# Stages two to six of a two-layer decoder in one block, with stage three rewritten and six weight pieces split inside it

## The reference, cut to what matters

```python
# stage three: one dense product, and one of four rank-8 LoRA experts per token
h = layernorm(x)
logits = h @ gate_w.T + expert_bias
e = argmax(logits)                              # one expert per token
x = x + h @ W_up.T + (h @ lora_A[e].T) @ lora_B[e].T
# stage four: a gated polynomial of seven terms and a gated feed-forward of width 1248
h = layernorm(x)
x = x + sum over d of value_d(h) @ W_down[d]    # 7 terms, then 10 blocks of silu(h Wg) * (h Wu)
```

## Time and profile before

| | before |
|---|---|
| median of 3 runs | 1293.69 us |
| the profiled execution | 1293.84 us, span 1291.9 us |
| TensorE busy | 1138.2 us, 88% of the span |
| VectorE, ScalarE, GpSimd busy | 749.5, 442.6, 399.7 us |
| mean granted TensorE clock | 0.935 |
| stage two | about 203 to 391 us |
| stage three | about 391.6 to 478 us |
| stage four | about 478.5 to 929 us |
| stages five and six | to 1291.9 us |

### The profile page before, as it was taken

The page is one execution under the profiler, slowest core; times in us unless marked ns, Lnnn a source line. Parts: engine busy times, 40 slices in busy tenths (PEclk is TensorE's granted clock), DMA queues, the critical chain, the costliest instruction groups (busy, mean ns, idle before and its releaser), DMA issues.

```text
span 1291.9 us, 24210 instructions
## 1 busy us (share of the span) xinstructions
PE 1138.2 (88%) x9396; PEld 602.5 (47%) x9396; DVE 749.5 (58%) x1308; ACT 442.6 (34%) x773; POOL 399.7 (31%) x339
## 2 busy tenths in 40 slices
PE   6798986988887978898999999999978799999993
PEld 3454443666664434344344444444545444444441
DVE  6767774788886874635721531531379833646456
ACT  4565662555541113421111211211256532223230
POOL 2345485878820010009800000000043400415053
PEclk9886885999998998998999999999989999999997
DMA  6000100111101003422200000000000000000000
GB/s 219 3 3 2 28 2 27 41 39 41 36 3 40 0 10 100 137 75 75 68 1 1 1 0 0 0 1 1 1 10 9 1 1 1 17 16 32 0 33 33
DMA packets 28911, 35.73 MB, mean 28 GB/s; under 512 B 5850, under 2 KB 20467, under 8 KB 28692
## 3 DMA queue, kind: packets, MB, share of 16 engines
q1 hardware_dynamic: 27410, 34.40, 8.3%
q10 hardware_dynamic: 1410, 0.06, 0.1%
HBM read 30.10 MB, written 4.19 MB: 27 GB/s over the span
## 4 chain that ended last, share of the span: by engine, by line
PE 47%; DVE 10%; ACT 3%; issue 2%; POOL 1%; DVEq 0%; POOLq 0%; ACTq 0%
PE p_up L113 9%; PE p_up L114 8%; PE p_up L115 8%; PE p_y L113 7%; PE p_y L114 7%; PE p_y L115 7%; DVE e_den L2122 1%; ACT wd_hi L2171 1%; DVE e_top L2112 1%; PE p_up L107 1%; DVE d_xn L100 1%; DVE e_bias L2115 1%; DVE d_h_low L1848 1%; DVE d_term L1839 1%; DVE d_xt_low L156 1%
## 5 line engine op out<-in xcount | busy, mean ns | idle before, releaser
L1848 DVE TENSOR_TENSOR d_h_low<-d_hf,d_h_high 128x512 f16<-128x512 f32 (+1 forms) x40 | 32.9, 822 | 204.5 <-ACT d_h_high L1916 204.5
L113 PE MATMUL p_up<-d_xt_high,wd_hi 128*128 128x512 f16 (+1 forms) x352 | 134.4, 382 | 1.5 <-PE p_y L115 1.5
L114 PE MATMUL p_up<-d_xt_low,wd_hi 128*128 128x512 f16 (+1 forms) x352 | 134.4, 382 | 0.0
L115 PE MATMUL p_up<-d_xt_high,wd_lo 128*128 128x512 f16 (+1 forms) x352 | 134.2, 381 | 0.0
L113 PE MATMUL p_y<-wd_hi,d_h_high 128*128 128x512 f16 (+1 forms) x272 | 104.4, 384 | 8.9 <-DVE d_h_low L1848 8.9
L114 PE MATMUL p_y<-wd_lo,d_h_high 128*128 128x512 f16 (+1 forms) x272 | 104.6, 385 | 0.0
L115 PE MATMUL p_y<-wd_hi,d_h_low 128*128 128x512 f16 (+1 forms) x272 | 104.4, 384 | 0.0
L129 POOL TENSOR_SCALAR ve<-mv 128x4 f32<-128x4 f32 x8 | 2.3, 292 | 314.5 <-DVE mv L188 314.5
L165 ACT ACTIVATE d_sg<-p_up 128x512 f32<-128x512 f32 (+1 forms) x40 | 23.8, 594 | 211.8 <-PE p_up L115 211.8
L429 POOL TENSOR_TENSOR a_pt_low<-a_ex,a_pt_high 128x1024 f16<-128x1024 f32 x32 | 68.3, 2135 | 81.1 <-ACT a_pt_high L918 81.0
L2380 DVE TENSOR_TENSOR d_h_low<-d_hf,d_h_high 128x512 f16<-128x512 f32 x32 | 27.5, 859 | 71.0 <-ACT d_h_high L2469 71.0
(11 more groups left out here) (327 smaller groups left out, 2988.7 us busy)
## 6 DMA issues: line engine op xcount, KB each, us to landing
wd_raw<-in_w_d SPq DMA_DIRECT2D x16, 616.0 KB, 3.7
wd_raw<-in_w_f SPq DMA_DIRECT2D x8, 578.0 KB, 3.7
X<-in_x SPq DMA_DIRECT2D x4, 1024.0 KB, 12.3
wd_lo<-in_ctx_t SPq DMA_DIRECT2D x128, 32.0 KB
out_x<-wd_raw SPq DMA_DIRECT2D x16, 256.0 KB, 2.0
wd_lo<-in_ctx SPq DMA_DIRECT2D x32, 64.0 KB, 2.4
wd_raw<-in_w_c SPq DMA_DIRECT2D x1, 1096.0 KB, 12.5
wd_hi<-in_Wo SPq DMA_DIRECT2D x1, 1024.0 KB
```

What stands on the lines that cost most here:

```text
L113: nc.tensor.matmul(ps, st[0], mv[0], start=start, stop=False)
L114: nc.tensor.matmul(ps, st[0], mv[1], start=False, stop=False)
L115: return nc.tensor.matmul(ps, st[1], mv[0], start=False, stop=stop)
L1848: nc.vector.tensor_tensor(hid[1][0:n, d % NH, :], value, hid[0][0:n, d % NH, :], ALU.subtract).then_inc(h_ready, 1)
```

## The change

Stages two to six become one block (`stages_bcdef`), with shared buffers and PSUM banks, and the loops of GpSimd and SP in stage two and of all engines in stage three are written out.

- **Stage two's end.** GpSimd makes rstd and -mean x rstd for stage three chunk by chunk inside stage two (`rstd_next`). ScalarE normalises stage three's tiles 0 and 1 at n = 28 and 30, TensorE transposes them ahead of the last `attend`, VectorE makes their low halves ahead of the last `norm_o`.
- **Stage three** (`part_c`). Normalisation moves to ScalarE (one activation with scale and bias). The gate has five operations for eight. z becomes f16 in high, high and low parts (ScalarE `high_z`, VectorE `low_z`), 96 columns, is transposed by one f16 matmul with an identity, copied by ScalarE (`copy_z`) and multiplied with an f16 lora of high, low and high rows: one pass for delta. TensorE's order is turn_z(t-1), trans(t+1), delta(t-1), products(t).
- **Six weight pieces of stage four** are split in stage three, after t = 2, 4, ..., 12: ScalarE writes the high half and then scales the raw piece in place (`high_first`), GpSimd subtracts (`low_first`). SP fetches pieces 0 and 1 at the end of stage two's fetches.
- **Stage three's end.** VectorE normalises stage four's tiles 0 and 1 at t = 14 and interleaves the rest with the last updates; TensorE's transposes (`turn_next`) stand between its last steps.
- **Stage four.** The ten other pieces are split at d = 2, 4, 6 and 7 to 13, behind the d's value on both engines and no longer ahead of it. Two normalisations of the next chunk come at d = 13 and 14, the other two ahead of all low halves. Stage five's folding of weights moves behind up(0), its first keys behind up(1).
- **Stage six** has the same new order of `prepare`, two normalisations at f = 5 and 6.

```diff
+EARLY = (2, 4, 6, 8, 10, 12)
...
+                def rstd_next(c):
+                    tiles = slice(TC * c, TC * c + TC)
+                    pool.wait_ge(stats, TC * c + TC)
+                    pool.wait_ge(vb_ready, VB * (min(TC * c + 2 * TC, NT) + 2))
+                    rstd_steps(nc, pool, held, tiles, held.rs_c + 2 * c)
+                    pool.wait_ge(held.rs_ready, held.rs_c + 2 * c + 2)
+                    nc.gpsimd.tensor_tensor(held.nmr[:, tiles], held.mv[:, tiles, 0], held.rstd[:, tiles, 0],
+                                            ALU.mult).then_inc(held.nmr_ready, 1)
+                    pool.wait_ge(held.nmr_ready, 2 * c + 1)
+                    nc.gpsimd.tensor_scalar(held.nmr[:, tiles], held.nmr[:, tiles], -1.0, None,
+                                            ALU.mult).then_inc(held.nmr_ready, 1)
+                for c in range(1, NC):
                     for i in range(TC):
                         tile(c, i, True)
-
-            @block.vector
-            def _(v):
+                    rstd_next(c - 1)
+                rstd_next(NC - 1)
...
+                    if n == N + 1:
+                        p.c.low(v, 0)
+                        p.c.low(v, 1)
...
+                    if n in (N - 4, N - 2):
+                        p.c.norm(act, (n - N + 4) // 2)
...
+                    if n == N:
+                        p.c.trans(pe, 0)
+                        p.c.trans(pe, 1)
...
+    def gpsimd(pool, weights):
+        for c in range(NC):
+            for q, t in enumerate(EARLY):
+                if TC * c <= t - 2 < TC * c + TC:
+                    weights(q)
+            rstd_chunk(nc, pool, held, c, stats, held.rs_d + 2 * c)
...
+    def gate(v, t):
+        k = 4 * t
+        v.wait_ge(aux_ready, t + 1)
+        nc.vector.scalar_tensor_tensor(logit[:], p_aux(t)[:, 0:EX4], 1.0 / (XS * WS), held.ebias[:],
+                                       ALU.mult, ALU.add).then_inc(gated, 1)
+        v.wait_ge(gated, k + 1)
+        nc.vector.tensor_reduce(top[:, 0:1], logit[:], AX.X, ALU.max).then_inc(gated, 1)
+        v.wait_ge(gated, k + 2)
+        nc.vector.scalar_tensor_tensor(pick[:], logit[:], top[:, 0:1], held.rank[:],
+                                       ALU.is_equal, ALU.mult).then_inc(gated, 1)
+        v.wait_ge(gated, k + 3)
+        nc.vector.tensor_reduce(top[:, 1:2], pick[:], AX.X, ALU.max).then_inc(gated, 1)
+        v.wait_ge(gated, k + 4)
+        nc.vector.scalar_tensor_tensor(
+            z32[:], pick[:].rearrange("p (e b) -> p e b", b=1).broadcast_to([128, EX4, R8]), top[:, 1:2],
+            p_aux(t)[:, EX4:CG].rearrange("p (e r) -> p e r", e=EX4), ALU.is_equal, ALU.mult).then_inc(zp_ready, 1)
+
+    def low_z(v, t):
+        v.wait_ge(zh_ready, t + 1)
+        nc.vector.scalar_tensor_tensor(zcat[:, t % 2, 2 * RZ:3 * RZ], z32[:].rearrange("p e r -> p (e r)"),
+                                       ZS / (XS * WS), zcat[:, t % 2, 0:RZ], ALU.mult, ALU.subtract).then_inc(zl_ready, 1)
...
+        for t in range(NT):
+            if t:
+                update(v, t - 1)
+            gate(v, t)
+            if 1 <= t < NT - 1:
+                low(v, t + 1)
+            low_z(v, t)
+            if t == NT - 2:
+                norm_next(0)
+                norm_next(1)
+            if t:
+                measure(v, t - 1)
+        low_next(0)
+        norm_next(2)
+        low_next(1)
+        norm_next(3)
+        update(v, NT - 1)
+        low_next(2)
+        low_next(3)
+        measure(v, NT - 1)
...
+    def norm(act, t):
+        act.wait_ge(held.nmr_ready, 2 * (t // TC) + 2)
+        if t >= 2:
+            act.wait_ge(t_ready, t - 1)
+        nc.scalar.activation(xn[:, t % 2, :], held.X[:, t, :], ACT.Identity, bias=held.nmr[:, t:t + 1],
+                             scale=held.rstd[:, t, 0:1]).then_inc(xn_ready, 1)
+
+    def high(act, t):
+        act.wait_ge(t_ready, t + 1)
+        if t >= 2:
+            act.wait_ge(out_ready, t - 1)
+        nc.scalar.activation(xt[0][:, t % 2, :, :].rearrange("p k n -> p (k n)"), p_t(t), ACT.Copy,
+                             scale=XS).then_inc(hi_ready, 1)
+
+    def high_z(act, t):
+        act.wait_ge(zp_ready, t + 1)
+        if t >= 2:
+            act.wait_ge(zt_ready, t - 1)
+        nc.scalar.activation(zcat[:, t % 2, 0:2 * RZ].rearrange("p (a n) -> p a n", a=2),
+                             z32[:].rearrange("p e r -> p (e r)").rearrange("p (a n) -> p a n", a=1)
+                             .broadcast_to([128, 2, RZ]), ACT.Copy, scale=ZS / (XS * WS)).then_inc(zh_ready, 1)
+
+    def copy_z(act, t):
+        act.wait_ge(zt_ready, t + 1)
+        if t >= 2:
+            act.wait_ge(out_ready, t - 1)
+        nc.scalar.activation(zt[:, t % 2, :], p_zt[0:3 * RZ, :], ACT.Copy).then_inc(zc_ready, 1)
...
+        for t in range(1, NT):
+            copy_z(act, t - 1)
+            if t + 1 < NT:
+                high(act, t + 1)
+            else:
+                high_next(0)
+            high_z(act, t)
+            if t + 2 < NT:
+                norm(act, t + 2)
+            if t in EARLY:
+                weights(EARLY.index(t))
+        high_next(1)
+        copy_z(act, NT - 1)
+        for i in range(2, TC):
+            high_next(i)
...
+    def turn_z(pe, t):
+        if t == 0:
+            pe.wait_ge(ident_ready, 1)
+        pe.wait_ge(zl_ready, t + 1)
+        if t:
+            pe.wait_ge(zc_ready, t)
+        nc.tensor.matmul(p_zt[0:3 * RZ, :], zcat[:, t % 2, :], ident_h[:], start=True, stop=True).then_inc(zt_ready, 1)
+
+    def delta(pe, t):
+        if t == 0:
+            pe.wait_ge(lora_lo, 1)
+        pe.wait_ge(zc_ready, t + 1)
+        nc.tensor.matmul(p_out(t), zt[:, t % 2, :], held.lora[0:3 * RZ, :], start=False, stop=True).then_inc(out_ready, 1)
+
+    def tensor(pe, turn_next):
+        products(pe, 0)
+        for t in range(1, NT):
+            turn_z(pe, t - 1)
+            if t + 1 < NT:
+                trans(pe, t + 1)
+            else:
+                turn_next(0)
+            delta(pe, t - 1)
+            products(pe, t)
+        turn_next(1)
+        turn_z(pe, NT - 1)
+        turn_next(2)
+        delta(pe, NT - 1)
+        turn_next(3)
...
-        beside = {0: 3, 1: 4, 3: 5, 4: 6, 5: 7, 6: 8, 7: 9, 8: 10, 9: 11, 10: 12, 11: 13, 12: 14, 13: 15}
...
+        beside = {2: 6, 4: 7, 6: 8, 7: 9, 8: 10, 9: 11, 10: 12, 11: 13, 12: 14, 13: 15}
...
+            def low_first(pool, q):
+                part = slice(PD * q, PD * q + PD)
+                if q == 0:
+                    pool.wait_ge(*held.b_done)
+                pool.wait_ge(wd_scaled, q + 1)
+                nc.gpsimd.tensor_tensor(held.wd_lo[:, part], raw[:, q % 2, :], held.wd_hi[:, part],
+                                        ALU.subtract).then_inc(wd_split, 1)
+
+            def high_first(act, q):
+                part = slice(PD * q, PD * q + PD)
+                act.wait_ge(wd_in[q % 2], 16 * (q // 2) + 16)
+                nc.scalar.activation(held.wd_hi[:, part], raw[:, q % 2, :], ACT.Copy, scale=WS).then_inc(wd_high, 1)
+                act.wait_ge(wd_high, q + 1)
+                nc.scalar.activation(raw[:, q % 2, :], raw[:, q % 2, :], ACT.Copy, scale=WS).then_inc(wd_scaled, 1)
...
 
+                    norm(c, 2)
+                    norm(c, 3)
                     for i in range(TC):
-                        v.wait_ge(t_ready, TC * c + i + 1)
-                        norm_tile(nc, held, xn[:, i % 2, :], TC * c + i).then_inc(xn_ready, 1)
-                        if i:
-                            low(v, nc, c, i - 1, hi_ready, xt_ready, xt, p_up)
...
+                        if d in weights:
+                            low_weights(weights[d])
+                        if not last and d in (DND - 4, DND - 3):
+                            norm(c + 1, d - DND + 4)
```

More of the change, by code:

```diff
@@ L382, in _ @@
                 fetch(held.ebias[:], row(a["expert_bias"]).broadcast_to([128, EX4]), par_c)
-                fetch(held.lora_b[:], a["lora_B"], par_c)
+                for r in range(3):
+                    fetch(held.lora_raw[32 * r:32 * r + 32, :], a["lora_B"], par_c)
                 for c in range(1, NC):
@@ L1245, in stage_b, with sync @@
         rs_at = held.rs_steps = held.rs_steps + 2
-        with nc.Block() as block:
-            @block.sync
-            def _(sp):
+        held.rs_c = rs_at
+        held.rs_steps += 2 * NC
+        held.b_done = v_ready, VW + N
+        if True:
+            def sync(sp):
                 def fetch(c, i):
@@ L1726, in part_d @@
+def part_d(nc, held, a, es, c_part):
     if True:
@@ L1771, in sync @@
             def sync(sp):
+                e = d.e
+                for q in range(2):
+                    sp.dma_start(raw[:, q, :], a["w_d"][:, PD * q:PD * q + PD]).then_inc(wd_in[q], 16)
                 e.fetch_weights(sp)
@@ L1916, in values @@
                         nc.scalar.activation(hid[0][0:n, d % NH, :], value, ACT.Copy).then_inc(hh_ready, 1)
-                for q in before[:2]:
```

(11 more changed lines are left out.)

460 lines of the change are left out of this document (201 added, 259 removed).

## The result

The changed kernel takes 1253.28 us (median of 4 runs, 1251.37 to 1257.22) where the kernel before, beside it, took 1293.66: a ratio of 0.9689, 95% interval 0.9656 to 0.9721. Five more runs of it later had a median of 1257.12 (ratio 0.9732, 0.9706 to 0.9757). The forecast was 1258.6, faster.

A forecast was written before the change was run, and what follows sets the result against it. TensorE was taken as saturated inside stage three and, but for waits, in the chunks of stages four and six, idling in seams. Terms -19.1 - 8.0 - 6.2 + 7.8 - 9.75 = -35.25 took 1293.84 to 1258.6 us; range 1246 to 1275.

The forecast's parts named there:

- Seams into and out of stage three: TensorE's idle time between stages two and three, and three and four, shrinks: -9.1 and -12.7 us.
- The low clock that I kept at stage four's start: Seam three to four: 12 matmuls were still assumed to run at half clock when stage four starts.
- Stage three: TensorE's period per plain tile falls from 4.60 to 3.72 us; the stage, without piece costs, takes 60.5 us: -14.1.
- Pieces on ScalarE: Stage three: each of six weight pieces delays the copy of z and so delta by 2.1 us: +12.6.
- GpSimd: Stage three: its subtract holds VectorE's gate step and pushes delta by 0.7 us, six times: +4.2; bounds nothing and 15.
- The addition of stage two that gave the lower bound: X + b_o on VectorE beside busy GpSimd never took over 0.81 us, so GpSimd's subtract might cost nothing.
- Chunk 0: Stage four's first chunk: waits for h_low vanish as six pieces are gone: -8.0 us, between 0 and 8.8.
- Seam of chunks 0 and 1: Stage four: two normalisations come ahead, the two left take 1.9 us each beside GpSimd; 14.5 becomes 8.3: -6.2.
- Chunk 1: Stage four: GpSimd's stage-six pieces slow more VectorE operations, so the downs end later: +7.8 us, bounds 0 and 12.
- Later seams: Chunks 1 to 2, 2 to 3 and stage six's three seams: last transposes end 1.95 us earlier each, -9.75.
- clock drops behind the six waits: Rival: each of stage three's six waits drops TensorE to 1.2 GHz, 2.5 us each; 1273.6 us, chance 0.19.
- Cheap pieces: Rival: stage three's pieces cost ScalarE 1 not 2.1, GpSimd's subtract nothing, chunk 1 only 4; 1244 us, chance 0.12.

The follow-up runs named there:

- e3: Changed kernel with delta and VectorE's update moved back behind the products of the next tile in stage three; 1252.14 us, ratio 0.9704 to the kernel before.
- e6: Changed kernel with ScalarE's two instructions per early piece parted over two tiles' idle time, GpSimd's subtract waiting for the low half of z; 1244.30 us (0.9620).
- e9: Changed kernel with the edits of e6 and e4 together; 1228.64 us, median of 5 (0.9518 to the kernel before).
- e2: Changed kernel with GpSimd's subtract of an early piece waiting for VectorE's low half of z of the next tile; 1258.24 us (0.9755).
- e5: Changed kernel with the edits of e3 and e2 together, and tile 14's statistics behind stage four's low halves; 1247.78 us (0.9652).
- e1: Changed kernel with three of the six early pieces (3 to 5) put back into stage four's first chunk; 1250.89 us (0.9697).
- e10: The changed kernel run once more, code unchanged; median 1257.12 us (ratio 0.9732 to the kernel before).
- e4: Changed kernel with GpSimd's stage-six weight pieces held until VectorE made the d = 6 hidden values of chunks 1 and 2; 1242.48 us (0.9616).
- e7: Changed kernel with stage six's normalisations back in the old order, each ahead of the low half of the tile before; 1259.26 us (0.9758).

## Why the prediction was right

**Seams into and out of stage three:** right in size and in kind (-9.8 and -12.4). The low clock that I kept at stage four's start did not come in either profile of the changed kernel; it came in e3 and e6. By the forecast's own 12 matmuls x 0.21 it is worth 2.5 us, and e6 and e9, which have the same code there, differ in chunk 0 by 3.2. That is enough for the 2.3 by which chunk 0 beat its term, so this part of the agreement in the sum is chance.

**Stage three:** the plain tile of 3.72 came at 3.70. Without what its pieces cost the stage would be 77.1 - 16.3 = 60.8; forecast 60.5, and e6 shows 61.4 with pieces at 0.1. **Pieces on ScalarE:** 2.0 of 2.1. The cause, the copy of z queued behind the piece, is shown by e6 beside e2: every instruction stays, only ScalarE's two move. **GpSimd:** 0.78 in the first pair and 0.72 in the others, of 0.7, and the value taken between bounds of nothing and 15 us was the right one. e2, e3 and e5 bear it out: the pick step, the low half of z, the 8-column copy each end with the subtract, whichever the subtract meets. The addition of stage two that gave the lower bound was read wrongly. It too was held, but only by the tail of a short instruction: 7 of the 16 additions took 0.72 to 0.81 and ended 0.54 to 0.55 behind GpSimd's, of which less than 0.3 us was left when they began. The longest, in the kernel before, beside the second of two GpSimd instructions, which ends at 365.93:

```profile
365.66 0.81 DVE L1370 TENSOR_TENSOR X<-X,b_o 128x512 f32<-128x512 f32 x1
364.51 1.42 POOL L1315 TENSOR_TENSOR wd_lo<-wd_lo 64x256 f16<-64x256 f32 x2
```

Two others began with 0.3 to 0.4 left of a longer GpSimd instruction and took 0.69; why they were not held is open.

By the Trainium skill ("SBUF — State Buffer", Who interferes with whom) a VectorE instruction with two SBUF inputs contends with a GpSimd one that reads SBUF, and so does one in a two-port mode, which a `tensor_scalar` can enter; one with at most one SBUF input outside these modes does not. The trace agrees for the first and the last (the update of X, with its other input in PSUM, took 0.69 beside the subtract at 397.58 as elsewhere); that e5's copy, a `tensor_scalar`, ran in such a mode no row shows.

**Chunk 0:** -10.3 for -8.0. Beside the clock the step has a gap in its reasoning: it put the gain down to six pieces being gone, and e1 shows that three of them are worth 1.5. Whether the other three carry the rest is not known.

**Seam of chunks 0 and 1:** -4.2 for -6.2. The two normalisations took 3.81 beside GpSimd, which is the forecast's 1.9 each in sum but not in kind: the first took 0.53 (GpSimd's multiply, begun half a microsecond ahead of it, took 4.03 where its like take 3.14), the second, begun at 566.38, 3.35, held until the multiply was done. VectorE and GpSimd:

```profile
565.92 3.81 DVE L103 TENSOR_SCALAR d_xn<-X,mv,rstd 128x512 f32<-128x512 f32 x2
565.42 4.03 POOL L138 TENSOR_SCALAR wd_raw<-wd_raw 128x1156 f32<-128x1156 f32 x1
```

What the step left out is the clock behind TensorE's wait for the second: down(16)'s 12 products took from 570.28 to 574.55, 4.3 us for 2.6, and the window 570 to 575 shows 0.66. That is 1.7 of the missing 2.0.

**Chunk 1:** +6.8 for +7.8, by four waits of 9.0 in place of two; with the clock's fall in e10 it is +8.5. e4 takes GpSimd's pieces away from there and the waits vanish with them, which shows the cause. **Later seams:** 1.6 each for 1.95 (e7 shows three of them as the order's own). The last two transposes still wait 0.44 for the third normalisation (TensorE at 684.71), which can start only when tile 0 is turned.

**Rivals:** clock drops behind the six waits are no cost here, 0 of 12 in two profiles, but real: e2 had two. The forecast gave this rival 0.19; as the same waits can go either way, its staying away is in part luck. "Cheap pieces" is wrong as a reading and right as a possibility, since e6 makes them so. The median of all nine runs, 1256.18, lies 2.4 us from the forecast; that the sum comes within 0.5 is in part luck too, since the parts in the table miss by 4.5 in all one way and by 4.0 the other.

## What to carry to other kernels

Price a moved instruction by what stands behind it in its engine's queue, not by its length: 2.45 us of ScalarE cost TensorE 2.0 in one place and 0.1 split over two idle gaps. GpSimd beside VectorE costs by what it meets, so hold its work until VectorE has little that can be held (e4: 14 us for two waits of GpSimd) and place it behind the last such instruction of a chain. And when a pair of profiles differs in code that wasn't touched, compare from a milestone behind it and repeat both kernels before explaining it.
